# Where the opening pieces, the last strip's local branch and the first parts of the rows' stage stand in a fused attention and transform layer

## The reference, cut to what matters

```python
win = xh.reshape(B, H // WS, WS, W // WS, WS, C).transpose(0, 1, 3, 2, 4, 5).reshape(-1, L, C)
qkv = (win @ qkv_w.T + qkv_b).reshape(-1, L, 3, HEADS, HD).transpose(2, 0, 3, 1, 4)
attn = softmax(einsum('bhld,bhmd->bhlm', q, k) * SCALE + bias[None])
out = einsum('bhlm,bhmd->bhld', attn, v).transpose(0, 2, 1, 3).reshape(-1, L, C) @ proj_w.T + proj_b
x_lpe = (conv2d(x, lpe_w, groups=C, pad=1) + lpe_b.reshape(1, C, 1, 1)) * lpe_scale * noise_mask
freq2 = dct2(x_attn_img + x_lpe)
gate = sigmoid(5.0 * (abs(freq2) - freq2.mean(axis=(2, 3), keepdims=True)))
y = batchnorm(conv2d(x + idct2(freq2 * gate), fr_w), bn2_g, bn2_b)
return gelu(y)
```

## Time and profile before

| | |
|---|---|
| median of 3 runs | 8457.01 us (8455.17 to 8464.24) |
| the profiled execution's own time | 8434.64 us |
| its span | 8432.9 us |
| TensorE's mean granted clock | 0.955 |
| TensorE, VectorE, ScalarE, GpSimd busy | 7852.1, 5507.1, 5152.9, 2724.1 us |

### The profile page before, as it was taken

The page is one execution under the profiler, slowest core; times in us unless marked ns, Lnnn a source line. Parts: engine busy times, 40 slices in busy tenths (PEclk is TensorE's granted clock), DMA queues, the critical chain, the costliest instruction groups (busy, mean ns, idle before and its releaser), DMA issues.

```text
span 8432.9 us, 251395 instructions
## 1 busy us (share of the span) xinstructions
PE 7852.1 (93%) x84778; PEld 5905.1 (70%) x84778; DVE 5507.1 (65%) x20355; ACT 5152.9 (61%) x17097; POOL 2724.1 (32%) x3673
## 2 busy tenths in 40 slices
PE   9998999999999999999999999999999999999920
PEld 8997676867776777767686777677776777676810
DVE  4555788468855886488747884588648874888410
ACT  5554776457754775377646775577547764776434
POOL 1120443224431443144323443244314431443200
PEclk9999999899999999999999999999999999999965
DMA  7653000110003000200021000200020002000189
GB/s 121 108 97 62 16 22 13 51 59 22 15 16 98 15 22 16 91 16 22 23 68 38 15 16 28 85 22 16 16 91 22 22 16 91 15 22 10 46 355 407
DMA packets 386808, 485.86 MB, mean 58 GB/s; under 512 B 249616, under 2 KB 352528, under 8 KB 369296
## 3 DMA queue, kind: packets, MB, share of 16 engines
q1 hardware_dynamic: 369488, 393.67, 16.2%
q0 software_dynamic: 16192, 77.49, 2.3%
HBM read 319.45 MB, written 151.66 MB: 56 GB/s over the span
## 4 chain that ended last, share of the span: by engine, by line
PE 63%; issue 21%; POOL 9%; DMA 4%; DVE 1%; POOLq 1%; ACT 1%; SPq 0%; DVEq 0%; ACTq 0%
PE ps L983 55%; PE ps L1122 4%; POOL work L441 4%; POOL work L476 3%; DMA AH<-y_scratch 2%; PE ps L1167 2%; DMA out<-AH 2%; PE ps L1119 1%; POOL work L438 1%; PE ps L1120 1%; POOL work L426 1%; POOLq L473 0%; POOL work L432 0%; DVE work L827 0%; ACT AH L685 0%
## 5 line engine op out<-in xcount | busy, mean ns | idle before, releaser
L568 ACT ACTIVATE work<-work 128x144 f32<-128x144 f32 x5120 | 2043.1, 403 | 23.1 <-DVE work L794 13.6
L983 PE MATMUL ps<-work 32*32 32x144 f32 (+3 forms) x32902 | 1711.2, 300 | 68.9 <-issue 30.7
L827 DVE SCALAR_TENSOR_TENSOR work<-xs,lw,work 128x570 f32<-128x570 f32 (+1 forms) x2048 | 1604.8, 820 | 0.0
L794 DVE CUSTOM_DVE_ANT_0 work<-ps,negbias 128x144 f32<-128x144 f32 x5120 | 1246.8, 302 | 494.2 <-issue 407.9
L983 PEld LDWEIGHTS ps<-work 32*32 32x32 f32 (+2 forms) x32902 | 966.9, 127 | 657.8 <-issue 567.2
L438 POOL TENSOR_TENSOR work<-work 128x80 f32<-128x80 f32 x1024 | 471.0, 460 | 2840.0 <-DVE work L801 2827.1
L441 POOL TENSOR_TENSOR work<-work 128x640 f32<-128x640 f32 x1024 | 1286.7, 1257 | 0.0
L983 PE MATMUL ps<-work,wqkv 128*128 128x288 f32 x4096 | 1269.6, 434 | 17.8 <-DVE work L794 11.4
L568 ACT ACTIVATION_READ_ACCUMULATOR work<-work 128x1 f32 x5120 | 971.2, 190 | 0.0
L983 PEld LDWEIGHTS ps<-work,wqkv 128*128 128x128 f32 x4096 | 721.6, 192 | 274.4 <-issue 24.2
L983 PE MATMUL ps<-dct,AH 96*96 96x97 f32 (+1 forms) x7168 | 800.0, 264 | 9.7 <-ACT AH L501 9.2
(11 more groups left out here) (130 smaller groups left out, 11846.4 us busy)
## 6 DMA issues: line engine op xcount, KB each, us to landing
work<-in_x SPq DMA_DIRECT2D x128, 576.0 KB, 5.4
xs<-in_x SPq DMA_DIRECT2D x64, 1152.0 KB, 5.2
AH<-in_x SPq DMA_DIRECT2D x192, 384.0 KB, 3.4
y_scratch<-AH SPq DMA_DIRECT2D x192, 384.0 KB, 2.6
AH<-y_scratch SPq DMA_DIRECT2D x64, 1152.0 KB, 22.8
out<-AH POOLq DMA_DIRECT2D x64, 1152.0 KB, 18.1
xs<-in_x SPq DMA_DIRECT2D x112, 96.0 KB, 5.1
bias_scratch<-in_rpb_rev POOLq DMA_DIRECT2D x144, 4.5 KB, 2.1
```

Source lines behind the costliest of these rows:

```text
L568: o = act.activation(sp[t % 4][:, c, :], sp[t % 4][:, c, :], ACT.Exp, scale=-1.0, bias=mn[t % 4][:, c:c + 1], accum_out=den[t % 4][:, c:c ...
L794: v.tensor_tensor_reduce(out=sp[t % 4][:, c, :], in0=psS[c], in1=negbias[:, t % 2, c, :], scale=1.0, scalar=BIG, op0=ALU.add, op1=ALU.min, ...
L827: v.scalar_tensor_tensor(dst[:, ct, :, w0:w1], xs[par][:, ct, y0 + dy:y0 + dy + HS, w0 + dx - 1:w1 + dx - 1], lw[:, ct, tap:tap + 1], dst[ ...
L983: return nc.tensor.matmul(o, l, r, start=start, stop=stop)
```

## The change

Four things change.

1. **The opening.** Eight pieces instead of seven are made in it, in banks 0, 1, 4, 5, 6, 7, 4, 5 (`first_banks`). The scores of step 0 come behind piece 2, those of step 1 behind piece 4, those of step 2 behind piece 5, and pieces 6 and 7 last. On VectorE the last group's statistics, their aggregation and the copies that keep them are spread between the scores (`last_stats`, `gathered`, `kept`). Step 0 of a first strip then makes piece 8 alone, where it made 7 and 8.
2. **The last strip's local branch.** Its 36 tap steps are spread over steps 0 to 13. Its second half is written to `xs[0]`.
3. **Early turns.** The transposes of the tail's rows 0 to 3 (`turn`) are taken out of the tail: rows 0 and 1 stand ahead of the transposes of step 15, row 2 ahead of and row 3 behind the last `attend`.
4. **Two early parts.** The first half of the channels of `zrows(0)` and `zrows(1)` (`zpart(0, 0)`, `zpart(1, 0)`) stands ahead of the last two `i1`.

```diff
+        first_banks = (0, 1, 4, 5, 6, 7, 4, 5)
...
+            if head and t == 0:
+                return [8]
...
-        def taps_at(t):
+        def taps_at(t, last):
+
+            if last:
+                return [divmod(k, 18) for k in range(36 * t // 14, 36 * (t + 1) // 14)] if t < 14 else []
...
+        def branch(s, half):
+
+            return xs[0][:, :, 0:HS, :] if s == NS - 1 and half else lpe[(2 * s + half) % 3]
...
+                        piece_out(3)
+                        piece_out(4)
                         exps(0)
+                        piece_out(5)
                         exps(1)
                         piece_out(6)
+                        piece_out(7)
...
-                        for t in range(3):
-                            scores_out(t)
+                        scores_out(0)
+                        beside[0]()
+                        scores_out(1)
                         recip(0)
+                        beside[1]()
+                        scores_out(2)
                         recip(1)
+                        beside[2]()
...
+                    attention(b + 1)(0, 0, first=True, beside=(last_stats, gathered, kept))
...
-                        pe.wait_ge(S["piece_out"], n * (NP * NPC) + HG)
                         pe.wait_ge(S["q_pad"], b * 6 + 6)
-                        for t in range(3):
-                            before_scores(t)
...
+                        scores_made(0)
+                        piece(3)
+                        freed()
+                        piece(4)
+                        scores_made(1)
+                        piece(5)
+                        scores_made(2)
+                        piece(6)
                         before_scores(3)
-                        piece(6)
+                        piece(7)
                         few_scores(3)
...
+                        if last and t == NT - 1:
+                            pe.wait_ge(S["a_row"], n * WS + 1)
+                            turn(n, 0, 0, par)
+                            turn(n, 1, 1, par)
                         transposes(t)
...
+                        turn(n, 2, 2, par)
                         before_attend(NT - 1)
                         attend(NT - 1)
                         attend_few(NT - 1)
+                        turn(n, 3, 3, par)
...
-                    if q >= 1:
+                    if 1 <= q < NCH - 1:
                         i1(q - 1)
...
+                zpart(0, 0)
+                i1(NCH - 2)
+                zpart(1, 0)
                 i1(NCH - 1)
```

More of the change, by code:

```diff
@@ L539, in attention, with strip @@
             def attention(b):
-                def strip(s, par, head=False, last=False, first=False, between=((lambda: None),) * NPC):
+                def strip(s, par, head=False, last=False, first=False, between=((lambda: None),) * 3):
                     n = b * NS + s
@@ L600, in strip @@
                             o_out(t - 2)
-                        made = pieces_at(t, last)
+                        made = pieces_at(t, last, head)
                         for i in made[:1]:
@@ L672, in image @@
                     still = lambda: None
-                    attention(b + 1)(0, 0, first=True, between=(still, y_late(0), y_late(1), still, still, still))
+                    attention(b + 1)(0, 0, first=True, between=(still, y_late(0), y_late(1)))
             attention(0)(0, 0, first=True)
@@ L783, in attention, with strip @@
             def attention(b):
-                def strip(s, par, head=False, last=False, first=False):
+                def strip(s, par, head=False, last=False, first=False, beside=((lambda: None),) * 3):
                     n = b * NS + s
@@ L813, in lpe_step @@
                     def lpe_step(half, k):
-                        dst = lpe[(2 * s + half) % 3]
+                        dst = branch(s, half)
                         ct, tap = k % 2, taps_order[k // 2]
@@ L869, in strip @@
                             scores_out(t + 3)
-                        steps = taps_at(t)
+                        steps = taps_at(t, last)
                         r = None if head else row_at(t)
@@ L1057, in attention, with strip @@
             def attention(b):
-                def strip(s, par, head=False, last=False, first=False, between=((lambda: None),) * NPC):
+                def strip(s, par, head=False, last=False, first=False, between=((lambda: None),) * 3, freed=lambda: None):
                     n = b * NS + s
@@ L1172, in row, with scores_made @@
                         last.then_inc(S["row_ps"], 1)
+                    def row(m, r, bank, side):
+                        turn(m, r, bank, side)
+                        project(m, r, bank, side)
                     if first:
+                        def scores_made(t):
+                            before_scores(t)
+                            score(t, signal=False)
+                            few_scores(t).then_inc(S["scores"], 1)
                         for i, beside in enumerate(between):
```

81 lines of the change are left out of this document (46 added, 35 removed).

## The result

The changed kernel takes 8344.67 us in the median of four runs (8338.81 to 8383.08), beside 8456.09 us for the kernel before (8440.67 to 8464.24, four runs). The ratio is 0.988 with a 95% interval of 0.9859 to 0.99: 1.2% faster. The forecast was 8370 us with a range of 8325 to 8420. The profiled execution took 8347.10 us, its span is 8345.4 us and its mean granted clock 0.963, where before had 8434.64 us and 0.955.

A forecast was written before the change was run, and what follows sets the result against it. TensorE was taken to be busy almost throughout, so its waits and low clock count. Early parts 42, openings 30, first image 2 and tails 13 sum to 87 us: 8457 - 87 = 8370 us, range 8325 to 8420.

The forecast's parts named there:

- The early parts: End of transforms and rows' stage: filled waits save 1.2 to 1.4 us an image, the clock more; 42 us in all.
- The opening: Seven openings at 36.2 us against 40.54, nearly all from the clock, 7 us still low in each; 30 us.
- the wait behind `gathered`: Opening, ahead of piece 7: TensorE waits 1.6 us, and the clock was expected to fall there still.
- The page's rule that I weighed: Opening: frequent short idle times make the clock go back and forth; nothing gained there, 57 us in all instead of 87.
- The last strip and tail: Strip's steps 0 within half a microsecond; tails gain four fifths of the 16.5 us of clock falls, 13 us.
- VectorE paces the tail, so only the first row's turn counts: Tail: VectorE is busy nearly all of its twelve rows, so early turns save 0.4 us an image.
- The taps' step: Last strip: four more tap steps in steps 0 to 10 cost 0.5 to 1 us; together 0 within half a microsecond.
- The first image: The first image's opening was to add some 2 us of gain.
- The transforms: Untouched, mean 151.9 us, falls seem to hang on small time shifts; counted as nothing, bounds -27 to +75 us.
- the opening falls as before: Rival: the clock falls at the new wait behind `gathered` and stays low as long; 30 us lost, 8400 us, chance 0.2.
- the early parts leave the clock: Rival: the `h_out` wait remains and the rows' stage begins low; only 10 of 42 us come, 8402 us, chance 0.1.
- All falls vanish: Rival: the opening stays at full clock too and gives 51 us; 8348 us, chance 0.12.

The follow-up runs named there:

- unrolled_sigmoid: The changed kernel with the sigmoid's table loaded early, under the tail, and the loop over images written out, so nothing branches back; 8279.55 us, ratio 0.9797.
- open_only: The kernel before with the changed opening alone, VectorE's order in it included; 8423.23 us, ratio 0.9961.
- gathered_late: The changed kernel with the aggregation (`gathered`) moved behind the third scores on VectorE; 8346.68 and 8382.50 us, ratio 0.989.
- sigmoid_fill: The changed kernel with the sigmoid's table loaded early and four matmuls that nobody reads behind the tail's last row; 8268.47 us, ratio 0.9776.
- all_three: The changed kernel with the image loop written out, the sigmoid's table loaded early and four idle matmuls behind the tail; 8219.54 us, ratio 0.9718.

## Why the prediction was right, and where it was not

**The early parts** were right in size (42 us forecast, 43.7 measured) and in kind. The 1.4 us an image for filling the waits with the halves' own work measured 1.2 to 1.4, and the clock gave 32.6 to 34 of the 43.7 us. The clean stage was put at 102.3 us with the old work in it and at 100.9 without, and is 102.27 and 101.10.

**The opening** gave 40.0 us instead of 30. Half of the surplus is the seventh opening: I gave all seven 36.2 us, and the one without a branch back took 31.36. The other half is 0.8 us in each of the six others. The wait ahead of piece 7 measured 0.91 us, not 1.6. That was a slip in my sum: 1752.95 and `recip(0)`, `gathered` (1.47 us) and five scores (1.2 us) give about 1755.8 for the end of the third set, not 1756.5. The branch back, taken over as 1.11 us from the earlier trace rows, measured 2.30. The 33.2 us for an opening at full clock came out right all the same (34.75 us less its low time at 0.43 is 33.2), by luck: `score(3)` starts 19.8 us behind the last `z_out`, not 18.9, and what follows it would take 13.4 us at full clock, not 14.3. The low time was 3.5 to 7.2 us in the six and none in the seventh, not 7: with the clock at 0.95, twice what it lacks to 1.00 of 34.75 us is 3.5 us. Three of the seven openings (34.75, 34.74 and 31.36 us) are shorter than the 35 to 38 us that I had named as the sign.

The step of the opening's working that failed is the one that has the clock fall at the wait behind `gathered`. It falls at the branch back and not without it: the seventh opening of the changed kernel has that wait, of 0.91 us, no branch and no fall, and in unrolled_sigmoid, with a wait of 0.79, no opening has one. Whether the branch's wait would be enough without the two short waits ahead of it, no run shows. The order of the work is worth more than the 1 us that I gave it where no branch follows: the seventh opening before, 37.00 us with 6.7 low, is by estimate 34.1 at full clock, and 31.36 after. In the other six the longer branch takes over 1 us of that back. What I had as the upper bound, 7 x 7.3 us for no fall, kept the branch: with it gone the sum is 219.24 us, 64.6 below before.

The page's rule that I weighed (the Trainium skill, "TensorE: Matmul & The Clock Gate", "A second HAM failure mode: psum-queue depth-cycling") would, as I read it, have given nothing from the opening as long as short waits remain. Here the measurement decides against that: in unrolled_sigmoid two waits of 0.49 and 0.79 us remain, and the clock stays at 1.00. The falls followed the wait of 2.30 us. A page of the Trainium skill that bears on this wait is "Runtime: NRT & Kernel Launch", section "Instruction fetch mechanics": a taken branch to instructions that are not at hand makes the engine fetch them first. By that rule, the trace agrees: TensorE (2.30 us) and ScalarE (2.47 us) wait for "issue" at the same place, and the wait goes with the loop. That fetching is what the wait consists of, the profile does not show.

**The last strip and tail** gave 24.7 - 1.0 = 23.7 us instead of 13. The mis-sized step is "VectorE paces the tail, so only the first row's turn counts". In the first tail before, TensorE's turns and projections follow one another without a gap:

```profile
1460.96 0.38 PE L1167 MATMUL ps<-eye,work 128*96 128x128 f32 x2
1461.18 1.03 PE L983 MATMUL ps<-wproj,work 128*96 128x256 f32 x4
1462.05 0.38 PE L1167 MATMUL ps<-eye,work 128*96 128x128 f32 x2
```

VectorE's timeline in the first tail of the changed kernel:

```profile
1449.50 0.48 DVE L859 SCALAR_TENSOR_TENSOR work<-ps,work,pb 96x256 f32<-96x256 f32 x1 [2.83 <-PE ps L1017]
...
1450.46 0.45 DVE L859 SCALAR_TENSOR_TENSOR work<-ps,work,pb 96x256 f32<-96x256 f32 x1
...
1451.40 0.45 DVE L859 SCALAR_TENSOR_TENSOR work<-ps,work,pb 96x256 f32<-96x256 f32 x1
...
1455.25 0.48 DVE L859 SCALAR_TENSOR_TENSOR work<-ps,work,pb 96x256 f32<-96x256 f32 x1
...
1456.33 0.48 DVE L859 SCALAR_TENSOR_TENSOR work<-ps,work,pb 96x256 f32<-96x256 f32 x1
```

The first rows follow each other at about 0.94 us and the later ones at 1.08. A row is 1.08 us because TensorE's turn and projection take that long; where the turns are made already, VectorE is quicker. So a clean tail is 1.0 us shorter (17.89 to 16.87), not 0.4, which is 8 us over eight: 0.4 us from the first row's earlier start, as forecast, and 0.6 from the quicker rows. The falls, 16.5 us, all went, where I had counted four fifths. VectorE's rate of 0.94 us was not in any row I had read: its busy time hid that it was fed at 1.08. The taps' step was right in size (+1.0 us for the eight strips). That they have a part in the tail's clock, as I had it, no run shows: the turns alone keep the clock high.

**The first image** gave 8.1 us instead of 2. open_only has all of it (859.7), so it is the opening's. I had no stage for it and took a guess below one mean opening's gain.

**The transforms** took 27.5 us back in the profiled execution, within my bounds, and their mean of 155.3 us stays just inside the 148 to 156 that I had named. The forecast's argument, that falls hang on small shifts in time, was neither shown nor refuted: open_only changed nothing there and has 43 us more, but runs of one kernel differ by as much. What the falls start from was in reach and I did not look for it: two waits at the start of the stage, 1.19 us for the last tail row and 1.66 us behind the table's load in the kernel before (1.20 and 1.66 after). With both edits against them all falls there went. Which images then have a long fall and which a short one is open.

**Of the rivals**, "the opening falls as before" and "the early parts leave the clock" did not come. "All falls vanish" did not come either, but the time it gave, 8348 us, is nearer to the median (8344.67) than mine, for another reason. My 8370 us took over from before that the median lies 22 us above the profiled execution, and in the changed kernel it lies 2 us below.

Also open is why the branch back takes 2.30 to 2.63 us here and 0.73 to 1.40 before. In gathered_late it grew as the wait ahead of it shrank, so that a part of it seems to end at a fixed time after something else; no run shows after what.

## What to carry to other kernels

Where the same instructions take different times in different images, compare the clock of the stage first: some 33 of the 44 us of the early parts, and 16.5 of 24.7 in the tails, were the clock's and not the work's. Fill the waits of TensorE with work that is due anyway, ahead of a stage that wants the full clock. If there is none, four matmuls an image that nobody reads were worth 55 us in the medians, once the table's load was moved (8323.69 to 8268.47); without that move no gain could be told. And an engine's busy time does not say that it sets the pace; the distance from one of its rows to the next, with its feeder taken away, does.

## What was not expected of the hardware

- The clock fell to 1.2 GHz in stretches whose longest single wait was 1.66 us, at the start of the transforms, and 0.67 us, at the start of the rows' stage before. It stayed at 2.4 GHz behind single waits of 0.65 and 0.91 us with work on both sides. The length of the longest wait alone does not say whether it falls.
- The branch back of the image loop cost 2.30 to 2.63 us of waiting and the low clock behind it, and the loop also 3.6 us an image in steps 3 to 112, where TensorE has no branch; there it waits nine times, 3.0 us in all, for nothing that the profile shows: 512.6 us written out, 516.2 in the loop. The last image, which is outside the loop, has 512.6 in both kernels.
- The scatter from run to run went with the transforms' falls. The changed kernel's four runs span 44 us, those of sigmoid_fill 4.7, of all_three 4.9.
